# Folding the experts' output and gate weights: two experts at a time, half-filled products side by side in the array, each result in its own PSUM bank

## What is computed

```python
for e in range(wq.shape[0]):              # 4 experts
    ...
    o = jnp.einsum('bhqk,bhkd->bhqd', attn, v)
    o = o.transpose(0, 2, 1, 3).reshape(b, s, h)
    outs.append(o @ wo[e].T)
fused = jnp.concatenate(outs, axis=-1)
gate = jax.nn.silu(fused @ w_gate.T)
value = fused @ w_up.T
return gate * value
```

## Time and profile before

| | |
|---|---|
| runs | 1117.25, 1114.33, 1114.12 us |
| median of the three | 1114.33 us |
| the profiled execution's own time | 1112.48 us |
| its span (first to last instruction) | 1110.8 us |
| TensorE, mean granted clock | 0.993 of full speed |
| busy: PE, PEld | 1069.5, 868.9 us |
| busy: DVE, ACT, POOL | 722.5, 763.2, 570.6 us |

### The profile page before, as it was taken

One profiled execution on the slowest core, in us unless ns is written; L12 is line 12 of the kernel. 1 busy time (PEld: TensorE's weight loads), 2 busy tenths in 40 slices (PEclk: granted clock), 3 DMA queues, 4 the chain that ended last, 5 costly groups with the idle time before them and its releaser, 6 DMA issues.

```text
span 1110.8 us, 34055 instructions
## 1 busy us (share of the span) xinstructions
PE 1069.5 (96%) x13103; PEld 868.9 (78%) x13103; DVE 722.5 (65%) x2256; ACT 763.2 (69%) x3370; POOL 570.6 (51%) x859
## 2 busy tenths in 40 slices
PE   6999998999999999999999999999999999999998
PEld 4788886777777465358888888888888888888577
DVE  8666566666766214367887878888888878877201
ACT  2356556777787435548988889888888888887231
POOL 2156666454455676436655465565465565465200
PEclk9999998999999999999999999999999999999999
DMA  8100603000000000010000000000000000000000
GB/s 273 29 5 2 135 3 79 1 2 1 2 1 1 1 1 1 1 51 2 3 3 3 2 3 3 3 3 3 3 2 3 3 3 2 3 3 3 11 22 32
DMA packets 35056, 19.66 MB, mean 18 GB/s; under 512 B 24656, under 2 KB 32336, under 8 KB 34896
## 3 DMA queue, kind: packets, MB, share of 16 engines
q1 hardware_dynamic: 34752, 17.00, 5.8%
q10 hardware_dynamic: 144, 0.49, 0.1%
HBM read 14.93 MB, written 1.77 MB: 15 GB/s over the span
## 4 chain that ended last, share of the span: by engine, by line
PE 88%; DVE 6%; ACT 3%; POOL 1%; issue 1%; DVEq 0%; POOLq 0%
PE banks L1750 8%; PE banks L1821 8%; PE banks L1758 6%; PE banks L1837 5%; PE banks L1532 5%; PE banks L1809 4%; PE banks L1856 4%; PE banks L2202 3%; PE banks L1814 3%; PE banks L2156 3%; PE banks L505 2%; PE banks L1258 2%; PE banks L1279 2%; PE banks L1861 2%; PE banks L1797 2%; PE banks L1844 2%
## 5 line engine op out<-in xcount | busy, mean ns | idle before, releaser
L2123 POOL TENSOR_TENSOR e_W<-e_W,e_RS 128x384 f32<-128x384 f32 x256 | 205.2, 827 | 233.0 <-DVE e_RS L1997 230.8
L1947 ACT ACTIVATE e_W<-banks,e_MX 128x128 f32<-128x128 f32 x768 | 270.1, 371 | 18.1 <-DVE e_MX L1983 18.1
L1947 ACT ACTIVATION_READ_ACCUMULATOR e_W<-banks,e_MX 128x1 f32 x768 | 161.2, 210 | 0.0
L1750 PE MATMUL banks<-XT,e_wqk 64*128 64x141 f32 x744 | 119.2, 295 | 0.0
L1750 PEld LDWEIGHTS banks<-XT,e_wqk 64*128 64x128 f32 x744 | 96.3, 188 | 18.1 <-issue 16.6
L1758 PE MATMUL banks<-e_wv,XT 128*128 128x192 f32 (+3 forms) x512 | 109.9, 344 | 0.6 <-DVE e_PT L2001 0.6
L1821 PE MATMUL banks<-ident,e_W 128*128 128x128 f32 x768 | 106.1, 274 | 1.1 <-POOL e_W L2123 0.8
L1506 POOL TENSOR_TENSOR f_W<-f_W,e_RS 128x423 f32<-128x423 f32 x64 | 56.3, 892 | 90.0 <-DVE e_RST L1485 79.7
L1941 ACT COPY e_PT<-banks 128x512 f32<-128x512 f32 x128 | 68.9, 588 | 40.6 <-PE banks L1821 40.3
L1983 DVE TENSOR_REDUCE e_MX<-banks 128x3 f32<-128x384 f32 x128 | 65.4, 552 | 41.4 <-PE banks L1809 41.4
L1821 PEld LDWEIGHTS banks<-ident,e_W 128*128 128x128 f32 x768 | 87.5, 143 | 2.3 <-DVE e_V L2010 1.0
(11 more groups left out here) (328 smaller groups left out, 2724.2 us busy)
## 6 DMA issues: line engine op xcount, KB each, us to landing
xp<-in_patches_dram SPq DMA_DIRECT2D x4, 768.0 KB, 9.2
H<-in_h_dram SPq DMA_DIRECT2D x1, 1728.0 KB, 13.2
out_dram<-H SPq DMA_DIRECT2D x6, 288.0 KB, 2.3
m_hid<-in_e_gu_dram SPq DMA_DIRECT2D x1, 1536.0 KB, 9.2
m_hid<-in_e_o_dram SPq DMA_DIRECT2D x4, 192.0 KB, 6.9
e_wqk<-in_e_qk_dram SPq DMA_DIRECT2D x8, 96.0 KB, 2.5
e_wqk<-in_e_qk_dram SPq DMA_DIRECT2D x24, 32.0 KB, 2.3
tokw<-in_tok_w_dram SPq DMA_DIRECT2D x1, 576.0 KB, 5.2
```

Of the source, the lines that this page charges most:

```text
L1750: return nc.tensor.matmul(bank[6][:, m * SEQ:(m + 1) * SEQ], ew[n % EXPERTS][0][0:rows_c, c, m * P:(m + 1) * P], XT[0:rows_c, c, tokens(n) ...
L1947: ex = nc.scalar.activation(W[n % 2][:, t, :], bank[i][:, x * P:(x + 1) * P], ACT.Exp, bias=MX[:, t:t + 1], accum_out=SM[n % 2][:, t:t + 1])
L2123: nc.gpsimd.tensor_tensor(x, x, RS[n % 2][:, 3 * i:3 * i + 3].unsqueeze(2).broadcast_to([P, 3, P]), ALU.mult).then_inc(s_nm, 1)
```

## The change

The order of the fold changes from expert by expert to two experts at a time, q = 0, 1. For output block 0: chunk 0 of both experts (two full products), then chunk 1 of both, expert 2q in rows 0 to 63 of the array and expert 2q+1 in rows 64 to 127. For output block 1: chunk 0 of both, 2q in columns 0 to 63 and 2q+1 in columns 64 to 127, then chunk 1 of both in the upper left and the lower right quarter. Each of the eight results has a bank of its own: banks 6, 7, 0, 1 for q = 0 and 2, 3, 4, 5 for q = 1.

Banks 0 to 5 hold the first layer of group 0, so the fold waits for its gelus 2, 4 and 6 (`s_mgl`) in place of its own evacuation, and the first layer of group 1 waits for the copies (`s_c`) that free its banks. For the odd experts the second chunk now lies in partitions 64 to 127, and their block 1 comes out there. So `load_late` issues 16 transfers where there were 5, one for each expert, chunk and matrix, and leaves out the padding.

```diff
--- before.py
+++ after.py
@@ -543,9 +543,11 @@
             load_up(sp, m_w1, d["f_w1"], w_ffn)
             sp.dma_start(m_w2[:, :, :], d["f_w2"]).then_inc(w_ffn, 16)
             for e in range(EXPERTS):
-                sp.dma_start(eo[:, e, :, :].rearrange("p c (h x) -> p (c h) x", x=HD),
-                             d["e_o"][e].rearrange("p c (h x) -> p (c h) x", x=HP)[:, :, 0:HD]).then_inc(w_fold, 16)
-            sp.dma_start(eg[:, :, :], d["e_gu"].rearrange("e p c n -> p e (c n)")).then_inc(w_fold, 16)
+                lo = e % 2 * C1
+                for c, at, n in ((0, 0, P), (1, lo, C1)):
+                    sp.dma_start(eo[at:at + n, e, c, :].rearrange("p (h x) -> p h x", x=HD),
+                                 d["e_o"][e][0:n, c, :].rearrange("p (h x) -> p h x", x=HP)[:, :, 0:HD]).then_inc(w_fold, 16)
+                    sp.dma_start(eg[at:at + n, e, c * 2 * C:(c + 1) * 2 * C], d["e_gu"][e][0:n, c, :]).then_inc(w_fold, 16)
             sp.wait_ge(sa_at, 2 * B)
             for e in range(EXPERTS):
                 for to, at, n in QK_PIECES:
@@ -557,27 +559,36 @@
 
         s_f, s_c = phase_sem(["folded", "fold_evacuated"])
 
+        FOLD_BANKS = ((6, 7, 0, 1), (2, 3, 4, 5))
+
+        def fold_part(dst, e, c, b, rows_b, start, stop):
+            lo, n = (e % 2 * C1, C1) if c else (0, P)
+            at = e % 2 * C1 if b else 0
+            return nc.tensor.matmul(dst[at:at + rows_b, 0:2 * C], eo[lo:lo + n, e, c, b * P:b * P + rows_b],
+                                    eg[lo:lo + n, e, c * 2 * C:(c + 1) * 2 * C], start=start, stop=stop,
+                                    tile_position=(lo, at), skip_group_check=True)
+
         def fold_products(pe):
-            pe.wait_ge(w_fold, 16 * (EXPERTS + 1))
-            for e in range(EXPERTS):
+            pe.wait_ge(w_fold, 16 * 4 * EXPERTS)
+            for q in range(EXPERTS // 2):
                 for b, rows_b in CH:
-                    u = e * 2 + b
-                    if u >= 2:
-                        pe.wait_ge(s_c, u - 1)
-                    for c, n in CH:
-                        mm = nc.tensor.matmul(bank[6 + u % 2][0:rows_b, 0:2 * C],
-                                              eo[0:n, e, c, b * P:b * P + rows_b],
-                                              eg[0:n, e, c * 2 * C:(c + 1) * 2 * C],
-                                              start=(c == 0), stop=(c == 1))
-                    mm.then_inc(s_f, 1)
+                    if (q, b) != (0, 0):
+                        pe.wait_ge(s_mgl, 4 * q + 2 * b)
+                    for c in range(2):
+                        for x in range(2):
+                            mm = fold_part(bank[FOLD_BANKS[q][2 * b + x]], 2 * q + x, c, b, rows_b, c == 0, c == 1)
+                            if c:
+                                mm.then_inc(s_f, 1)
 
         def fold_evacuate(act):
-            for e in range(EXPERTS):
-                act.wait_ge(s_f, 2 * e + 1)
-                nc.scalar.copy(gu_w0[:, e, :], bank[6][:, 0:2 * C]).then_inc(s_c, 1)
-                act.wait_ge(s_f, 2 * e + 2)
-                lo = e % 2 * C1
-                nc.scalar.copy(gu_w1[lo:lo + C1, e // 2, :], bank[7][0:C1, 0:2 * C]).then_inc(s_c, 1)
+            for q in range(EXPERTS // 2):
+                for x in range(2):
+                    act.wait_ge(s_f, 4 * q + x + 1)
+                    nc.scalar.copy(gu_w0[:, 2 * q + x, :], bank[FOLD_BANKS[q][x]][:, 0:2 * C]).then_inc(s_c, 1)
+                for x in range(2):
+                    act.wait_ge(s_f, 4 * q + x + 3)
+                    lo = x * C1
+                    nc.scalar.copy(gu_w1[lo:lo + C1, q, :], bank[FOLD_BANKS[q][2 + x]][lo:lo + C1, 0:2 * C]).then_inc(s_c, 1)
 
         def build_masks(pool):
 
@@ -1543,6 +1554,8 @@
                                 pe.wait_ge(s_nra, T3 + BACK_F)
                                 pe.wait_ge(s_nev, T3 + IN_F)
                                 pe.wait_ge(sf_o, 2 * B)
+                            if g == 1:
+                                pe.wait_ge(s_c, (4, 4, 5, 6, 8, 8)[m])
                             up_part(g, m, m, 0, 0, P, True, False)
                         if g == 0:
                             for k, i in enumerate(REST3):
```

## The result

| kernel | runs (us) | median |
|---|---|---|
| before | 1117.25, 1114.33, 1114.12, 1114.76 | 1114.55 |
| changed | 1107.62, 1103.24, 1104.02, 1104.05 | 1104.03 |

The account below looks back on a forecast made before the run. TensorE, busy 96% of the span, was taken as the bound; the fold's 13.02 us becoming 7.84 saves 5.2, all other terms cost nothing, so the median goes from 1114.33 to 1109.1 us, range 1106.5 to 1111.8.

Parts of the forecast that it names:

- The fold: TensorE's fold products, grouped by shape and paired, take 7.84 us instead of 13.02, a win of 5.2 us.
- the diagonal pair: Two 64*64 products on the array's diagonal in the fold: taken as overlapping, 0.79 us; 1.44 if serial.
- Rival A: Fold's column and diagonal pairs run serially: win 2.6 us, 1111.7; chance 5% both, 5% diagonal alone, 2% columns alone.
- Waits: In the fold, ping-pong evacuation waits go and waits for gelus 2, 4, 6 come; both cost nothing.
- evacuation: ScalarE's eight fold copies, 3.8 us, end by about 385.4; 1.6 us of slack, nothing paid.
- next stage: After the fold and first layer, transposes start at about 388.5 and `wide_down` moves earlier by the whole 5.2 us.
- loads: SyncE's 16 transfers instead of 5 take 9 to 38 us in an idle gap; cost nothing.
- Rival C: Clock falls to 1.2 GHz in the fold and group 1's first layer: 5.2 us lost, 1119.5; chance 3%.
- Rival D: The time is waited for elsewhere, at GpSimd's norms or ScalarE's evacuation: 1112 to 1114 us; chance 3%.
- the sum's last step: Whole kernel: from the profiled execution's 1107.3 us to the three-run median, 1.85 us higher, giving 1109.1.
- the range's low end: Whole kernel: 1106.5 us, from 1107.6 at the upper bound of 6.7 us won, with 1 more from the clock.
- rival B: Later clock falls, such as at 495 to 500, change: loss 1.7 us, 1110.8, chance 12%; gain 1.4, 1107.7.

Follow-up runs that it names:

- Experiment 4: Changed kernel with each expert's two chunks run back to back, so no pairs; fold 13.03 us, span 1110.9 us.
- experiment 5: Changed kernel with odd experts' block 1 also in columns 0 to 63; 128*64 pair 1.43 us, fold 9.12 us.
- r_pad: Changed kernel with eight more full products ahead of its fold; fold stretch 13.0 us, mean 1112.11 us, 0.9993 of the kernel before.
- e_alone: The kernel of Experiment 4: changed kernel without pairs, chunks of one expert back to back; fold 13.03 us, span 1110.9 us.
- r_after: Label not defined in the text; apparently the changed kernel run again without edit, first time: mean 1106.41 us, ratio 0.9948.
- r_after2: Label not defined in the text; apparently the changed kernel run again without edit, second time: mean 1106.27 us, ratio 0.9947.
- r_loads: The loads-only kernel: the change's loads and operands with the old fold order, banks and waits; mean 1112.12 us, 1.0003 of the kernel before.
- e_quads: Changed kernel with all four experts of a shape back to back, 64*64 products in four quarters; fold 6.51 us, mean 1105.48 us.

## Why the prediction was right and wrong

**The fold** came out as worked: 7.84 us in the sum, 7.84 in the chain. The two full products, the row pair and the column pair cost what the earlier trace rows gave, and the diagonal pair, for which the trace had nothing, 0.80 where the prediction took 0.79 between bounds of 0.79 and 1.44. Experiment 4 shows that the pairing and the grouping are the whole of it, experiment 5 that one kind of pair is worth 2 x 0.64 us.

**Rival A** fell with the diagonal pair. The Trainium skill (TensorE: Matmul & The Clock Gate, Part 3) lets a weight load overlap running products only where the row group differs, from which the prediction worked out serial column pairs. The trace does not agree: the pair in one row group took 0.79 us, against 1.43 when it shared its columns too.

**Waits, evacuation, next stage, loads** were all right: no wait was added to the chain, the last copy ended at 385.2 (forecast 385.4), `wide_down` moved to 393.0 (393.2, and 0.27 of the move is the earlier arrival at the fold), GpSimd caught up, and SyncE's 14.4 us lie between the 9 and 38 that were given. **Rival C** did not happen (1.00 in the fold). **Rival D** neither.

**What failed is the sum's last step and the range's low end.** "... so the median goes to **1109.1 us**" took the median of three runs, 1114.33, as the kernel's time, and "the clock can give a further 1" took rival B as one fall of one size at one place. The runs show a median of 1111.64 for the kernel before, so the base was 2.7 us too high, and falls that come and go at several places. In the profile of before they lie around 185 to 190 and 495 to 500, in that of after at 390 to 400 and at 35 to 45 (0.59 and 0.73 in its two windows of 5 us); the loads-only kernel has none of them. In other profiled executions the clock fell at 35 to 45, 165 to 170 and 495 to 505 (r_pad, e_alone), or at 180 to 195 (r_after, r_after2). The kernel before so spreads over 10 us, with a mean of 1112.3 and not 1114.3. Of the 2.8 us between the forecast and the changed kernel's mean over 32 runs, 2.0 is that base (1114.33 against the mean of 1112.31), and the rest the difference between 5.2 and 6.0, of which 0.3 is the slightly better clock. With the base at its mean the forecast is 1107.1; by medians it is 1111.64 - 5.2 = 1106.4, against the changed kernel's 1106.16. Around that, the median of four runs of one kernel can lie 2 to 4 us from its middle, and the difference of two such medians 4 to 5 us, so the low end of 1106.5 lay inside the scatter. The three runs shown, 1114.12 to 1117.25, and one profiled at 1112.48 were the hint: a spread of 4.8 in four numbers, of which I used 1.7. The first comparison's 10.5 us is thus 5.2 of fold, which is shown, and about 5 that a draw of four against four can give but that no run shows to be one.

**Open:** at an equal clock 5.6 us are left, 0.4 more than the fold's 5.2. The two traces without falls in between show 5.18 and no more, and the clock is listed to 0.001, which is 1 us of time, so this may be rounding; no run tells. The fall at 495 to 505 stands in three of the four profiled executions with a fold of 13.0 us (before, e_alone and, with its padding, r_pad; not r_loads) and in none of the eight with a shorter fold. So its place may hang on when the fold ends, though the mean clocks of the runs show no gain from that beyond the 0.3 us. What decides whether TensorE's clock falls at a place in one execution and not in the next was not tried either.

## What to carry to other kernels

Count a product's price from one weight load to the next, by shape: if each change of shape shows idle load time and the next stage of the same kernel runs the same shapes in pairs, the gain can be read off before anything is built, to a tenth of a us. Put products of a shape behind each other and place halves in different rows or different columns, each with its own bank, as here (whether the halves of a pair could share one was not tried). And ahead of any forecast in us, look how far the runs of one kernel scatter and how that goes with the clock: a gain of 5 us can be read in the chain at once, but takes dozens of runs to see in the times. Between two traces without a fall on the way it came out to 0.1 us here.

## What the runs showed of the hardware that was not expected

- Four 64\*64 products of 384 columns in the four quarters take 0.80 us together (e_quads), practically the price of one alone (0.78), with eight weight loads within 0.21 us.
- Two 128\*64 products in different columns overlap fully (0.79 us for both), and with the same columns not at all (1.43 us).
- A change of the array's shape costs 0.19 us before a 128-column product (0.84 - 0.65) and 0.14 us before a 64-column one (0.79 - 0.65), worked out from the load rows, whether the results go to one bank or to several, and with or without waits between (13.03 us in both cases).
- A fall of the clock behind TensorE's 1.9 us wait ahead of `wide_down` appears in the changed kernel's first profile (0.93 and 0.73) and costs 1.68 us there; in the loads-only kernel the same wait is followed by 1.00.
- Over 104 runs of two kernels, 1 us at the lower level costs 0.48 us of time by the fit, close to the 0.5 that it would cost were TensorE on the path all the time.
